# Two parts of eleven and five sequences, and the first part's tables and zeroed tails built in steps 67 to 75

## The reference

```
x = x + attention(layernorm(x))      # 16 heads of 8, 4 key/value heads, window of 32 keys,
                                     # rms-normed and rotated q and k, softmax, pair mix, Wo
h = layernorm(x)
logits = h @ router_w.T              # 8 experts
e1, e2, w1, w2 = two best experts of each token, weights by a jitter-masked softmax
x = x + sum over the two of w * (silu(h @ w_gate[e].T) * (h @ w_up[e].T)) @ w_down[e].T
```

## Time and profile before

| | |
|---|---|
| median of 3 runs | 601.63 us (601.54 to 603.01) |
| the profiled execution, its own time | 603.13 us |
| its span, first to last instruction | 601.3 us |
| PE / DVE / ACT / POOL busy | 531.7 (88%) / 446.0 (74%) / 332.9 (55%) / 337.1 (56%) us |
| granted TensorE clock, mean | 0.970 |

### The profile page before, as it was taken

One profiled execution on the slowest core, in us unless ns is written; L12 is line 12 of the kernel. 1 busy time (PEld: TensorE's weight loads), 2 busy tenths in 40 slices (PEclk: granted clock), 3 DMA queues, 4 the chain that ended last, 5 costly groups with the idle time before them and its releaser, 6 DMA issues. The chain is left out here.

```text
span 601.3 us, 20442 instructions
## 1 busy us (share of the span) xinstructions
PE 531.7 (88%) x6060; PEld 382.0 (64%) x6060; DVE 446.0 (74%) x1764; ACT 332.9 (55%) x1171; POOL 337.1 (56%) x468
## 2 busy tenths in 40 slices
PE   0599999899999999999984799999999999999970
PEld 0267787677777777777763466666666666666650
DVE  2569999999999999999999455646565555656553
ACT  1446776667767667767653455454544455444530
POOL 1222221866668766668754748264655655557655
PEclk9999999999999999999998599999999999999995
DMA  9512211332223322212231223244655554554543
GB/s 304 186 36 45 46 28 37 73 68 63 58 66 75 71 52 48 51 55 59 57 84 49 76 85 119 76 132 130 164 140 142 146 141 136 143 147 132 150 112 86
DMA packets 123530, 58.06 MB, mean 97 GB/s; under 512 B 53793, under 2 KB 118689, under 8 KB 123169
## 3 DMA queue, kind: packets, MB, share of 16 engines
q1 hardware_dynamic: 112640, 34.90, 23.6%
q0 software_dynamic: 8192, 16.79, 9.9%
q10 hardware_dynamic: 2592, 5.07, 2.2%
HBM read 28.14 MB, written 24.64 MB: 88 GB/s over the span
## 5 line engine op out<-in xcount | busy, mean ns | idle before, releaser
L1205 POOL DMA_INDIRECT expert_in<-xn,slot_r x128 | 127.5, 996 | 88.5 <-DVE slot_r L837 64.4
L1274 POOL DMA_INDIRECT ga<-expert_out,row_all x128 | 122.2, 954 | 92.4 <-DVE yb L1168 30.4
L653 PE MATMUL chb<-wgu,xbT 128*128 x288 | 151.1, 607 | 0.0
L1161 DVE TENSOR_TENSOR h<-sil,chb 128x256 f32<-128x256 f32 x144 | 60.6, 421 | 102.3 <-ACT sil L466 102.2
L381 ACT ACTIVATE pT<-chb 128x512 f32<-128x512 f32 x128 | 76.5, 598 | 83.6 <-DVE mx L854 49.2
L466 ACT ACTIVATE sil<-chb 128x256 f32<-128x256 f32 x144 | 55.4, 384 | 121.4 <-PE chb L653 121.4
L667 PEld LDWEIGHTS chb<-ident,h 128*128 128x128 f32 x288 | 40.5, 142 | 79.0 <-issue 42.5
L854 DVE TENSOR_REDUCE mx<-chb 128x8 f32<-128x512 f32 x128 | 85.4, 676 | 2.6 <-PE chb L577 2.1
L667 PE MATMUL chb<-ident,h 128*128 128x128 f32 x288 | 55.6, 275 | 1.5 <-DVE h L1161 1.4
L1229 POOL TENSOR_TENSOR tq<-t,rr 128x128 f32<-128x128 f32 x64 | 27.0, 421 | 48.7 <-issue 44.2
L596 PE MATMUL pp<-wp,xyT 128*128 128x272 f32 x128 | 50.2, 476 | 4.2 <-DVE t L939 2.6
(11 more groups left out here) (142 smaller groups left out, 1156.6 us busy)
## 6 DMA issues: line engine op xcount, KB each, us to landing
xb<-expert_in SPq DMA_DIRECT2D x144, 64.0 KB, 1.8
expert_out<-yb SPq DMA_DIRECT2D x72, 128.0 KB, 1.9
xa<-x SPq DMA_DIRECT2D x16, 256.0 KB, 3.1
out<-oo SPq DMA_DIRECT2D x32, 128.0 KB, 2.1
qk<-qk SPq DMA_DIRECT2D x64, 48.0 KB
wgu<-w_gu ACTq DMA_DIRECT2D x1, 2048.0 KB, 8.8
expert_in<-xn,slot_r POOLq DMA_INDIRECT x128
ga<-expert_out,row_all POOLq DMA_INDIRECT x128, 2.6
```

The costliest lines, as they stand in the source:

```text
L653: nc.tensor.matmul(chb[:, b % 2, :], xbT[:, b % 4, :], wgu[:, e, :], start=True, stop=True).then_inc(gu_done, 1)
L1161: nc.vector.tensor_tensor(h[:, b % 4, :], sil[:, b % 2, :], chb[:, b % 2, FF:2 * FF], ALU.mult).then_inc(h_ok, 1)
L1205: nc.gpsimd.indirect_dma_start(xs_dram, bass.IndirectOffsetOnAxis(ap=slot_r[:, q % 4, 2 * v + k:2 * v + k + 1], axis=0), xn2[:, t % 16, :] ...
L1274: nc.gpsimd.indirect_dma_start(ga[:, q % 2 * TPS + v, j, :], None, ys_dram[0:blocks * P, :], bass.IndirectOffsetOnAxis(ap=row_all[:, q * T ...
```

## The change

The first part is eleven sequences (`SPLIT` 12 to 11), the second five; the blocks are 96 and 48 instead of 104 and 40. `T_STEP` becomes 67, and the pieces of `places(0)` come after steps 67 to 70, six at a time. A new `T_TURN` of 73 is the step at whose head PE turns the columns. DVE runs three pieces of `tables(0)` after each of steps 73, 74 and 75. `past` is computed for four sequences at a time, the last piece for three (part 0) or one (part 1). SP writes three zeroed tails after its step 68, three after 69 and two after 70. POOL's wait for them moves with `SPLIT` from step 75 to step 71, and the count that SP waits for on the four scatter semaphores is written for part ends that four does not divide.

```diff
--- before.py
+++ after.py
@@ -30,7 +30,7 @@
 EXP, FF = 8, 256
 CAP = TOK + P
 SLACK = EXP * (P - 1) // P
-SPLIT = 12
+SPLIT = 11
 PARTS = ((0, SPLIT), (SPLIT, SEQS))
 NBS = tuple(2 * TPS * (q1 - q0) + SLACK + 1 for q0, q1 in PARTS)
 NBA, NB = NBS[0], sum(NBS)
@@ -57,7 +57,8 @@
 MEM = 8
 S_MOE = NT + L_PV
 QUICK = 6
-T_STEP, T_SLOT, T_COLS = 71, 22, 44
+T_STEP, T_SLOT, T_COLS = SPLIT * TPS + L_RT + 3, 22, 44
+T_TURN = T_STEP + 6
 
 
 def tile(s, lag):
@@ -296,24 +297,26 @@
             sp.wait_ge(zero_ok, 1)
             for n in range(SPARE):
                 sp.dma_start(xs_dram[EXP * CAP + n * P:EXP * CAP + (n + 1) * P, :], zero[:, :]).then_inc(c_zero, 16)
+            def clear_tail(part, e):
+
+                at = sp.value_load(tail[0:1, part, e:e + 1], min_val=0, max_val=EXP * CAP)
+                sp.dma_start(xs_dram[bass.ds(at, P), :], zero[:, :]).then_inc(tail_in, 16)
+
             for s in range(STEPS):
                 step(s)
-
-            def clear_tail(part, e):
-
-                at = sp.value_load(tail[0:1, part, e:e + 1], min_val=0, max_val=EXP * CAP)
-                sp.dma_start(xs_dram[bass.ds(at, P), :], zero[:, :]).then_inc(tail_in, 16)
+                if s == T_STEP + 1:
+                    sp.wait_ge(tail_ok, 1)
+                if T_STEP < s <= T_STEP + 3:
+                    for e in range(3 * (s - T_STEP - 1), min(3 * (s - T_STEP), EXP)):
+                        clear_tail(0, e)
 
             def dispatched(part):
 
                 sp.wait_ge(tail_in, (part + 1) * EXP * 16)
                 for n in range(4):
-                    sp.wait_ge(scat[n], PARTS[part][1] // 4 * TPS * 2 * 16)
+                    sp.wait_ge(scat[n], len(range(n, PARTS[part][1], 4)) * TPS * 2 * 16)
                 sp.wait_ge(tabs_ok, part + 1)
 
-            sp.wait_ge(tail_ok, 1)
-            for e in range(EXP):
-                clear_tail(0, e)
             sp.wait_ge(c_zero, SPARE * 16)
             dispatched(0)
 
@@ -630,7 +633,7 @@
                 last.then_inc(colsT_done, 1)
 
             for s in range(S_MOE):
-                if s == S_MOE - 1:
+                if s == T_TURN:
                     pe.wait_ge(v_ok, NT)
                     pe.wait_ge(t12_ok, NT)
                     turn_columns(0)
@@ -1131,10 +1134,10 @@
                 settled()
                 dve.wait_ge(rt_chain, q1 * RT_OPS)
                 for g in range(q0, q1, TPS):
-                    wide = [P, TPS, 2 * TPS, 2 * EXP]
-                    nc.vector.tensor_tensor(past[:, g:g + TPS, :, :],
-                                            slot_all[:, g:g + TPS, :].unsqueeze(3).to_broadcast(wide),
-                                            limits[:, g:g + TPS, :].unsqueeze(2).to_broadcast(wide), ALU.is_ge)
+                    z = min(g + TPS, q1)
+                    wide = [P, z - g, 2 * TPS, 2 * EXP]
+                    nc.vector.tensor_tensor(past[:, g:z, :, :], slot_all[:, g:z, :].unsqueeze(3).to_broadcast(wide),
+                                            limits[:, g:z, :].unsqueeze(2).to_broadcast(wide), ALU.is_ge)
                     yield
                 nc.vector.tensor_copy(jumps[:, q0:q1, 0], shifts[:, q0:q1, 0])
                 nc.vector.tensor_tensor(jumps[:, q0:q1, 1:], shifts[:, q0:q1, 1:], shifts[:, q0:q1, 0:2 * EXP - 1],
@@ -1148,10 +1151,12 @@
             work = places(0)
             for s in range(S_MOE):
                 step(s)
-                if T_STEP <= s < S_MOE - 1:
-                    some(work, 6 if s < S_MOE - 2 else SEQS * EXP)
-            work = tables(0)
-            some(work, 3)
+                if T_STEP <= s < T_TURN:
+                    some(work, 6 if s < T_TURN - 1 else SEQS * EXP)
+                if s == T_TURN:
+                    work = tables(0)
+                if s >= T_TURN:
+                    some(work, 3)
 
             def slot(s):
                 b = block_at(s, B_GU)
```

More of the change, by code:

```diff
@@ L298, in _ @@
                 sp.dma_start(xs_dram[EXP * CAP + n * P:EXP * CAP + (n + 1) * P, :], zero[:, :]).then_inc(c_zero, 16)
-            for s in range(STEPS):
-                step(s)
             def clear_tail(part, e):
@@ L305, in clear_tail @@
                 sp.dma_start(xs_dram[bass.ds(at, P), :], zero[:, :]).then_inc(tail_in, 16)
+            for s in range(STEPS):
+                step(s)
+                if s == T_STEP + 1:
[3 more added lines that the diff above has]
+                        clear_tail(0, e)
             def dispatched(part):
```

## The result

The changed kernel is slower: a median of 605.25 us (602.92 to 607.82, 8 runs) against 601.59 (599.82 to 603.01, 8 runs) for the kernel before; the ratio is 1.0066 with a 95% interval of 1.0044 to 1.0088. A second set, taken later, gave 606.32 against 602.90, 1.0045 (1.0021 to 1.0068). The ratios with their intervals are estimated from all the runs of a set, so they are not exactly the ratio of the two medians. The forecast was 602.8 and "no change", with a range of 599.9 to 605.0; the time lies just above it.

The account below looks back on a forecast made before the run. DVE was taken as the bound in steps 67 to 70, PE close behind. The terms +6.4 - 4.9 + 2.1 - 2.4 summed to +1.2 us, a median of 602.8 us, range 599.9 to 605.0.

Parts of the forecast that it names:

- Steps 67 to 70: Attention steps taking over `places(0)`: 6.79 us of DVE portions less 0.38 us of idle cover, +6.4 us.
- The upper end of 7.6: Most that `places(0)` could cost in its new steps, with 0.8 us for collisions of DVE and POOL.
- Steps 71 to 76: Attention steps freed of `places(0)`, -4.9 us, and given `tables(0)` behind 73, 74 and 75, +2.1 us.
- behind step 76: Handover to the slots: `tables(0)` no longer stands in front of the routing operations and `xn`, -2.4 us.
- Eleven and five: Expert slots under the new split: gathers, `rows(1)` and part 1's larger `places` and `tables` cost 0.
- Tail writes and early loads: SP's zeroed tails between k copies, and tables and block loads ready earlier for slot 3: both 0.
- (a): Rival, handover to the slots: the clock stays up, up to -4.5 us, 598.3 (600.5 with half); chance 0.13.
- a sign of being wrong: At the handover, the stretch at a granted 0.50 being over 2 us longer or shorter than before.
- (b): Rival, steps 75 and 76: the clock falls sooner, ahead of step 77, +2.5 us, 605.3; chance 0.12.
- (c): Rival: everything hides, DVE's portions meet unseen idle time and terms lie at low ends, -1.2 us, 600.4; chance 0.15.
- (d): Rival: tail writes hold up SP, the k copy is late, 1 us in each of three steps, 605.8; chance 0.05.

Follow-up runs that it names:

- pool_small: The changed kernel with POOL's three rotary operations of tiles 60 to 63 done on 8 columns, the rest left out; 604.75 us (one run).
- late_tables: The changed kernel with the turn back at step 76 and `tables(0)` behind step 76 and slots 0 to 2; 607.02 us, 1.0062 of the kernel before.
- after_slot27: The changed kernel with `places(1)` begun in slot 27 instead of 22; 605.12 us (one run).
- after_again: The changed kernel once more, unaltered, for a second execution's records; 606.32 us (12 runs), 1.0045 of the kernel before.
- late_tails: The changed kernel with the eight tail writes behind SP's last step, as before the change; 610.70 us, 1.0117 of the kernel before.
- before_deferred: The kernel before with part 0's limits, shifts, past and jumps moved from slots 0 to 2 to slots 8 and on; 601.88 against 603.50 us, 0.9984.
- deferred_slot27: before_deferred with `places(1)` begun in slot 27 instead of 22; 600.25 us against 602.88 for the kernel before, 0.9959.

## Why the prediction was wrong

**Steps 67 to 70, forecast +6.4, measured +7.5.** The mechanism was right, DVE bound and no cover, and the size was off. The portions last 2.12 + 2.15 + 1.9 + 1.52 = 7.7 us, not 6.8, and of the 0.38 us of idle time that I counted as cover only 0.2 was. The excess over the forecast's 6.79 us of portions is 0.9, all of it in the first two. The prediction had the number, 0.8 us for collisions, from line L946's longest instance, and set it aside because it "asks for a collision in each step". pool_small shows that the collisions are there: it takes 0.6 us from the stretch y 67 to y 68 and 0.5 from the next, which hold these two portions, and 0.4 from the third. The upper end of 7.6 is 6.79 + 0.8 with no cover at all; beside the 0.38 us of cover it would have been 7.2. So that 7.5 lies inside the bounds is partly luck. The Trainium skill ("SBUF — State Buffer", Who interferes with whom) says that a VectorE operation with two SBUF inputs and a GpSimd operation that reads SBUF exclude each other for the whole instruction; by it the upper end was the value to take, and the measured 7.5 agrees.

**Steps 71 to 76, forecast -4.9 and +2.1, measured -4.5 and +1.6, together right (-2.8 against -2.9); behind step 76, forecast -2.4, measured -2.2.** late_tables separates them. The stretch up to slot 3 comes to +2.4 us instead of +1.2, and the whole excess is the first term.

**"Eleven and five: 0" failed.** This term had been put at nothing. It measured +1.1 us and has two parts. One is slot 22, above: shown by after_slot27, where it disappears. The other is `rows(1)`. The prediction reasoned that it leaves the place in front of the gather at 551.24 and asked only whether the gather would wait. It did not ask whom POOL disturbs at the new place. after_again, POOL and DVE:

```profile
538.12 1.55 POOL L1257 TENSOR_TENSOR past<-past,jumps 128x640 f32<-128x640 f32 x1
539.74 2.19 POOL L1261 TENSOR_TENSOR past<-past 128x320 f32<-128x320 f32 x4
...
538.81 1.02 DVE L1179 SCALAR_TENSOR_TENSOR acc<-ga,w,xa 128x128 f32<-128x128 f32 x1
539.86 0.89 DVE L1183 SCALAR_TENSOR_TENSOR oo<-ga,w,acc 128x128 f32<-128x128 f32 x1
540.67 0.41 DVE L1166 TENSOR_TENSOR h<-sil,chb 128x256 f32<-128x256 f32 x1
```

The two combine operations take 1.91 us; the pair behind them, with POOL quiet, takes 0.34 and 0.35. `h` starts at 540.67, and PE's weight load for it stands waiting; the transpose of block 118 comes 1.93 us behind that of 117 and the next one 1.82 us later, instead of 1.64:

```profile
541.13 0.20 PEld L670 LDWEIGHTS chb<-ident,h 128*128 128x128 f32 x2 [0.91 <-DVE h L1166]
```

Before, the same collision was there, shorter:

```profile
547.04 1.28 POOL L1252 TENSOR_TENSOR past<-past,jumps 128x512 f32<-128x512 f32 x1
...
547.73 0.75 DVE L1174 SCALAR_TENSOR_TENSOR acc<-ga,w,xa 128x128 f32<-128x128 f32 x1
548.52 0.76 DVE L1178 SCALAR_TENSOR_TENSOR oo<-ga,w,acc 128x128 f32<-128x128 f32 x1
```

0.75 + 0.76 us, and PE had no gap. So the slack of a slot holds 1.5 us of combine and not 1.9. This second part is read from profiles alone; all ten profiles with eleven and five show it (65.8 to 66.2 us for blocks 100 to 140), and none of the six of this study with twelve and four (65.4 to 65.6). No run took `rows(1)` away.

**Tail writes and early loads.** Right that both are worth 0 as made; wrong on what would follow if the tails were late, where late_tails shows 4.7 us.

**The rivals.** (a), a clock that stays up, did not occur. The first profile of the changed kernel has its granted 0.50 for 17 us (327.1 to 344.1), over 3 us shorter than the 20.4 of before, which was a sign of being wrong; but the two later ones have 20.4 again, and before_deferred, with the old split, has 17.1. So the sign is one of the execution and not of the change. (b) had as its sign any half-clock operation of PE ahead of step 77. That came, but in steps 68 to 71, behind the waits that the portions made, which (b) had not priced and where it cost nothing. A fall in steps 75 and 76, as (b) priced it, stands in deferred_slot27's profile, with the old split:

```profile
319.00:323.00 4.00, 3.63 (x39) 2.69 (x40) 3.68 (x21) 1.36 (x3) 0.00 (x0) 0.55 0.01 1
```

y 71 to y 76 there takes 21.8 us instead of 20.3: +1.5, where (b) had 2.5. It is part of the spread between executions, since before_deferred, the same code up to slot 22, lacks it. None of the three profiles of the changed kernel had it, so the result does not rest on it. (c) did not occur. Nor did (d): PE waits for no k copy in these three profiles. The bounds of the terms, taken together, reached +5.6; the range was cut below that by weights, and the slot terms had no bounds at all, which is the graver fault.

## What to carry to other kernels

When work is moved, price it at the place where it lands: list what each other engine does there that shares something with it, and price also the work of another engine that changes its place as a consequence (here POOL's `rows(1)`), not only the transfer or wait that it used to stand in front of. Where a stage has slack, give the slack a number; "hidden" was true for 1.5 us per slot and false for 1.9. And with executions that differ by 3 us, compare stretches between equal events over two or three profiles of each kernel: the parts that belong to the kernel repeat to 0.1 us, and the total doesn't.

## What the runs showed of the hardware

A DVE cast of 1x8 elements took 1.47 us beside a POOL operation of 1.67 us (the first of the four merged in the row at 376.88), against 0.14 alone, and ended 0.02 us behind it: the length of this collision was set by the other engine's instruction. The granted clock fell after PE waits of 1.76 and 3.17 us, at the same steps in three executions; in late_tables, with the same code so far, it stayed up behind the 1.76 us and fell behind 1.85 and 1.81. And 28 extra transposes, put into PE's waits of four steps, restored the clock without giving back any time, since the engine that made PE wait was the bound. Where DVE had no such work, behind y 71 in pool_small, the same fall to 1.2 GHz made DVE wait 0.91 us for PE.
